# GCN passes of a graph-network stack: every sixth group, from the twelfth on, picked by TensorE in place of every seventh

## The reference, cut to what matters

```python
def gcn_conv(x, src, dst, W, b, n_nodes):
    h = x @ W.T
    ...
    msg = h[src] * norm[:, None]          # one row of 128 values for each edge
    out = jax.ops.segment_sum(msg, dst, num_segments=n_nodes)
    return out + b
h = gcn_conv(x, src, dst, W1, b1, n)
h = jax.nn.relu(graph_layernorm(h, g1, be1))
h = gcn_conv(h, src, dst, W2, b2, n)
```

## Time and profile before

| | before |
|---|---|
| median of 3 runs | 4421.98 us (4414.29 to 4436.6) |
| profiled execution, its own time | 4389.91 us |
| its span | 4387.9 us |
| pass 0: first gather | 970.0 us |
| pass 1: first gather to the end of group 103 | 1621.1 to 2158.2 us |
| pass 2: first gather to the end of group 103 | 2188.0 to 2727.1 us |
| mean granted TensorE clock, share of full speed | 0.772 |

### The profile page before, as it was taken

One profiled execution on the slowest core, in us unless ns is written; L12 is line 12 of the kernel. 1 busy time (PEld: TensorE's weight loads), 2 busy tenths in 40 slices (PEclk: granted clock), 3 DMA queues, 4 the chain that ended last, 5 costly groups with the idle time before them and its releaser, 6 DMA issues.

```text
span 4387.9 us, 52346 instructions
## 1 busy us (share of the span) xinstructions
PE 2793.6 (64%) x15364; PEld 2036.7 (46%) x15364; DVE 2080.7 (47%) x4427; ACT 1555.9 (35%) x3919; POOL 2371.9 (54%) x2449
## 2 busy tenths in 40 slices
PE   3177788872333356877767877557676774666667
PEld 2055556632222334555534554345555553455555
DVE  5033334641222345566546655235555663555557
ACT  2054444540000033333343333234454423444443
POOL 1745555116666636666366664335666534555653
PEclk9976666885555668899879988567888886887887
DMA  4322222131111112222122221345555424455541
GB/s 86 68 56 59 62 60 62 23 130 47 46 46 48 45 56 53 53 53 53 53 61 55 53 52 34 105 126 141 139 144 146 129 81 128 135 139 135 146 135 45
DMA packets 351656, 360.74 MB, mean 82 GB/s; under 512 B 125198, under 2 KB 274389, under 8 KB 351381
## 3 DMA queue, kind: packets, MB, share of 16 engines
q0 software_dynamic: 89600, 211.77, 18.4%
q1 hardware_dynamic: 255638, 143.69, 12.7%
q10 hardware_dynamic: 6148, 1.93, 0.3%
HBM read 327.08 MB, written 30.26 MB: 81 GB/s over the span
## 4 chain that ended last, share of the span: by engine, by line
PE 41%; another core or an unknown queue 21%; DVE 15%; issue 15%; ACT 3%; POOL 1%; DMA 1%; SPq 1%; DVEq 1%; ACTq 1%; POOLq 0%
PE QX L1368 20%; PE NU L1368 12%; PE MTB L1368 7%; DVE sums_transposed L834 3%; DVE extra_sums_transposed L834 2%; DVE gathered_rows L834 1%; DVE messages L834 1%; DVE query_key_products L834 1%; POOL gathered_rows L549 1%; PE MID L1368 1%; SPq L436 1%; DVE scan_scores L981 1%; ACT window_distance L698 1%; ACTq L601 0%
## 5 line engine op out<-in xcount | busy, mean ns | idle before, releaser
L532 POOL DMA_INDIRECT gathered_rows<-key_value_rows,src_index x832 | 829.6, 997 | 646.2 <-DVE messages L834 356.3
L834 DVE TENSOR_TENSOR sums_transposed<-sums_transposed,NU 128x512 f32 x624 | 425.7, 682 | 1140.7 <-remote 740.6
L549 POOL DMA_INDIRECT gathered_rows<-gcn_rows,src_index x720 | 684.5, 951 | 470.0 <-issue 194.6
L532 POOL DMA_INDIRECT gathered_rows<-gat_rows,src_index x416 | 397.0, 954 | 391.6 <-DVE messages L1008 191.1
L1368 PE MATMUL NU<-start_penalty,zero_weights 128*128 128x512 bf16 x624 | 278.5, 446 | 423.1 <-DVE sums_transposed L834 328.1
L549 POOL DMA_INDIRECT gathered_rows<-relation_rows,src_relation_index x416 | 400.9, 964 | 206.2 <-issue 123.8
L794 ACT ACTIVATE gathered_rows<-iota_window,dst_in_window_by_edge 128x128 f32<-128x128 f32 x832 | 265.1, 389 | 608.4 <-remote 445.0
L729 ACT ACTIVATE edge_node_onehot<-iota_window,dst_in_window_by_edge 128x128 f32<-128x128 f32 x1248 | 394.8, 387 | 155.1 <-remote 135.4
L1368 PEld LDWEIGHTS NU<-edge_node_onehot,messages 128*128 128x128 f32 x2496 | 414.0, 234 | 47.0 <-issue 26.5
L1368 PE MATMUL NU<-gathered_rows 128*128 128x128 f32 x2496 | 395.5, 310 | 56.5 <-issue 33.3
L1368 PE MATMUL NU<-edge_node_onehot,messages 128*128 128x128 f32 x2496 | 413.6, 318 | 24.7 <-issue 24.6
(11 more groups left out here) (294 smaller groups left out, 4357.0 us busy)
## 6 DMA issues: line engine op xcount, KB each, us to landing
query_window<-query_rows SPq DMA_DIRECT2D x832, 66.0 KB
dst_in_window_row<-dst_in_window SPq DMA_DIRECT2D x156, 256.0 KB
gathered_rows<-key_value_rows,src_index POOLq DMA_INDIRECT x832
relation_rows<-gathered_rows SPq DMA_DIRECT2D x25, 512.0 KB
gathered_rows<-gcn_rows,src_index POOLq DMA_INDIRECT x720
dst_in_window_row<-src_place_and_block SPq DMA_DIRECT2D x28, 256.0 KB
gathered_rows<-gat_rows,src_index POOLq DMA_INDIRECT x416
query_window<-gat_target_scores SPq DMA_DIRECT2D x416, 2.0 KB
```

Source lines behind the costliest of these rows:

```text
L532: pool.indirect_dma_start(out=rows_of(a, s)[:, t, :], out_offset=None, in_=a["table"], in_offset=bass.IndirectOffsetOnAxis(ap=srcI[:, TPG ...
L549: pool.indirect_dma_start(out=linear_rows(p["k"], k)[:, t, :], out_offset=None, in_=p["table"], in_offset=bass.IndirectOffsetOnAxis(ap=p[" ...
L834: return dve.tensor_tensor(o, x, y, op)
```

## The change

Every sixth group is picked instead of every seventh, and the first candidate of each pass, k = 5, is left out. Picked are k = 11, 17, ..., 101: 16 groups in each of passes 1 and 2 in place of 14, and 88 groups are gathered in place of 90. The picks follow groups 6 to 9, 12 to 15 and so on to 96 to 99; two steps out of six have no pick. The wait for `parts_ready` moves to the new first picked group.

```diff
-    TURN, LEAD = 7, 5
+    TURN, LEAD = 6, 5
...
         def by_matmul(p, k):
-            return p > 0 and k % TURN == TURN - 1
+            return p > 0 and k % TURN == TURN - 1 and k > TURN
...
                     if n >= 2:
                         dve.wait_ge(S["picked_psum"], n - 1)
-                    if t == 0 and k == TURN - 1:
+                    if t == 0 and k == 2 * TURN - 1:
                         dve.wait_ge(S["parts_ready"], 5 * p["k"])
```

## The result

| | before | after |
|---|---|---|
| median, 9 runs each, in turns | 4429.58 us | 4457.93 us |
| lowest to highest | 4414.29 to 4437.96 us | 4446.79 to 4468.08 us |
| profiled execution, its own time | 4389.91 us | 4467.57 us |
| pass 1, first gather to the end of group 103 | 537.1 us | 555.9 us |
| pass 2 | 539.1 us | 560.5 us |

The ratio is 1.0067, 95% interval 1.0052 to 1.0083: slower by 28 us. The forecast was slower, 4476 us, with a range from 4370 to 4535 us.

The account below looks back on a forecast made before the run. No engine fills the 35.3 us period: PE and DVE in turns take 30.3 us, holds 5.0. Opening 70 + 15 x 31.0 + ending 30.2 = 565.2 us a pass, +54 us on the median: 4476 us, range 4370 to 4535 us.

Parts of the forecast that it names:

- holds: Microseconds when a finished step's release reaches nobody: 5.0 us a period before, forecast 2.8 us, bounds 1.2 and 5.0.
- The period: Passes 1 and 2, first pick to next first pick: 31.0 us forecast, 28.2 us free plus 2.8 us of holds.
- the free stretch behind the fourth pick: From a period's fourth pick to the next first pick, without holds: 9.1 us becomes 7.0 us.
- rival 5: PE's clock stays up at a period's first pick, saving 1.7 us a period: 29.3 us, 4425 us in all; chance 0.08.
- The opening: First gather to first pick of passes 1 and 2: held until the ring is full, 70 us forecast.
- the hold's end: At the start of passes 1 and 2: the opening hold ends 10 to 15 us later than 56.5 us.
- The ending: Last first pick to the end of a pass: four fewer groups at 1.11 us, mean 30.2 us.
- The sum: Opening, 15 periods and ending: 565.2 us a pass against 538.1, +27 us a pass, +54 us in all.
- a sign of being wrong altogether: Passes 1 and 2 shorter than 537 and 539 us, or time changing outside of them.
- POOL's rhythm as the pace (1, 2): POOL sets a 29.4 us period: opening held, 4428 us, chance 0.12; no opening hold, 4368 us, chance 0.16.
- Rival 4: Holds stay at 5.0 us a period: period 33.2 us, +60 us a pass, 4542 us; chance 0.17.
- had rows waiting: Mid-pass, PE hardly ever waits for gathered rows as the ring is full; the argument against POOL's rhythm as the pace.

Follow-up runs that it names:

- r2: The changed kernel run once more, nothing else changed, on a chip without holds: ratio 1.0100 to the kernel before, median 3643.59 us.
- f1: The changed kernel with places and the first one-hot of a period made one step earlier on DVE: ratio 0.9925 to the kernel before.
- r1: The kernel before run once more, unchanged, on a chip without holds: ratio 0.9989, median 3602.24 us.
- e4: The kernel before with TURN = 52, so only groups 51 and 103 of a pass are picked: ratio 1.0326 to the kernel before.

## Why the prediction was right, and where its terms were off

**Direction** was right, and so was the mechanism for the changed kernel. The change takes load off POOL and puts it on PE and DVE, which were about the limit already; `r2` shows PE waiting for DVE and, in the 15 periods, never for rows, and `f1` shows that the gain on POOL exists once that wait is gone. For the kernel before the mechanism was shown to be incomplete: where nothing is held, POOL limits its pass too (see the rivals). The runs that show this all stand on chips without holds; for the chip of the forecast only the two traces speak.

**The period.** 31.0 us was forecast, 30.9 and 31.0 measured over all 15. That it came out so closely is luck in part: the first period was 8 to 12 us longer than forecast and the other 14 0.6 to 0.9 us shorter. Its parts: the free stretch behind the fourth pick, put at 7.0 us, is 6.9 in `r2`. The holds, which I had put at 2.8 us between bounds of 1.2 and 5.0, are what is left, 2.8 us in both passes: 30.08 less 28.2, with 1.65 us back in 8 of 14 periods for the quick first picks (0.94 us on average), and 30.43 less 28.2, with 5 of 14 (0.59 us). Nothing in the sum had fixed 2.8 within its bounds, so to hit it was luck. The mis-sized term is the clock. I had made it all (rival 5, 1.7 us in every period) or nothing, and took nothing; it was a third to a half. That is 13 us too much in pass 1 and 8 us in pass 2. The Trainium skill ("TensorE: Matmul & The Clock Gate", Part 1) has PE's clock fall with idleness and return with activity. The two levels are there: the granted clock is 1.00 over the quick pick at 1500.24 in `r2` and 0.67 over the first 2.4 us of the one at 1526.69. But the waits ahead of the two are the same, so the length of the waits alone didn't tell in advance which pick would be slow.

**The opening.** My reading that the hold's end moves by 10 to 15 us with the group that is held was wrong: it ended 56.3 us after the first gather in pass 1, the very time of the kernel before, and 62.3 us in pass 2, 5.7 us later than before. 64.7 and 68.3 us to the first pick came near 70 because of what follows. What I had not foreseen is the second hold, at 85 us in both passes, in which DVE waited 12.8 and 12.6 us. Opening and first period together were forecast at 101.0 and took 107.3 and 107.0 us.

**The ending** was 30.2 us by the old endings less four groups; it took 27.5 us. The old ones had holds in them: on the chip without holds `r2`'s is 27.3 us.

**The sum.** +54 us forecast; +18.8 and +21.4 us, together +40 us, in the two traces; +28 us between the medians, with an interval from 23 to 37 us. The clock accounts for 21 us of what I had too much, the ending for 5, and the first period takes 12 back. The step from 40 to 28 I can't place: the profiled execution of the kernel before lies 40 us below its median and that of the changed one 10 us above, and the two traces differ by 38 us outside of passes 1 and 2, where the code is the same. I had named a time that changes there as a sign of being wrong altogether; 18.1 of the 38 us lie ahead of the first gather of pass 1 (1639.17 against 1621.09), where nothing is changed yet, so this is scatter between executions at least in part. One trace of each is too few to say how much of such scatter falls in the passes. Adding a difference of traces to a median was fair, but its error is of that size, and my own range of the forecast, 4452 to 4512 us, allowed for little of it.

**The rivals.** POOL's rhythm as the pace (1, 2) did not decide in the changed kernel, yet it was nearer the truth than I made it: where nothing is held, it does set the pass of the kernel before (its gathers start over 452 us of 458). Rival 4, holds of 5.0 us, fell: they did shrink, to 2.8 us. That the longer pauses of POOL did it is my reading; no run shows it. I had given POOL's pace too little weight because PE "had rows waiting"; in `r1` PE has them waiting in every period as well, and the debt is paid at the end, in the 47 us ending. Rows that wait in front of PE in the middle of a pass are no proof that the gatherer is not the limit of the pass. A full ring is another thing: in `r1` POOL never pauses in passes 1 and 2, so its ring is never full there, while in the first trace it pauses about 40 times a pass.

**Holds.** What was shown: they depend on where the kernel runs. The kernel before took 4430 us in the first measurement and 3602 to 3609 us in the experiments, on four chips. The trace of `r1` has no wait at all that ends by "remote", in any stage; the first trace has 740.6 us of them on DVE's additions and 445.0 us on one line of ACT (L794). In these traces that word was the mark of a hold. What holds the releases stays open: chip, machine and whatever ran beside the kernel were not told apart. What `f1` does on a chip that has holds is open too.

## What to carry to other kernels

When a change moves work from one engine to another, add up both engines' own time for the whole pass, ending included; a change pays only up to the point where they cross, and here a wait of 1.8 us a period, for an operand made a step too late, had moved that point. Look for that wait first: taking it away turned 1.0100 into 0.9925, and turned the sign of another edit. And before an idle term of unknown cause goes into a sum, ask for a trace from another chip.

## What the runs showed of the hardware

The same program took 4430 us in one place and 3605 us in others, 19% less, at a mean granted clock of 0.772 against 0.817. Both are steady: the runs of the kernel before in one group of measurements lie within 0.7% of each other, here as there. PE in order of time in the changed kernel's second hold, where nothing stands between the matmuls of one pick, nor between those of one group:

```profile
1713.46 0.27 PE L1368 MATMUL NU<-gathered_rows 128*128 128x128 f32 x1 [1.84 <-issue]
1715.57 0.37 PE L1368 MATMUL NU<-gathered_rows 128*128 128x128 f32 x1 [1.83 <-issue]
1717.68 0.48 PE L1368 MATMUL QX<-query_window,gathered_rows 128*128 128x384 bf16 x1 [1.74 <-issue]
1719.08 0.48 PE L1368 MATMUL QX<-query_window,gathered_rows 128*128 128x384 bf16 x1 [0.93 <-issue]
```

They start 1.4 to 2.1 us apart, against 0.16 us in a quick pick (ten in 1.80 us), and from 1723.98 on, 3.7 us into POOL's pause of 4.20 us, they follow each other without gaps again, first at the pace of the lower clock (five in 1.75 us). So in this hold more than releases is late: the starts of matmuls that wait for no semaphore are spread too. That gathering without a pause is the cause is not shown; the two go together in time. On a chip without holds 408 gathers go out back to back in 509.6 us (`e4`), and no wait in that trace ends by "remote".
